# Head products copied raw and split inside the first FFN; W1 and W2 loaded where their low halves lie

## The chip, the cores and the metric

One core of a Trainium2 chip runs one program. The metric is the device time of one execution in microseconds (us), the median of several runs. The engines are named as in the profile: PE (TensorE), DVE (VectorE), ACT (ScalarE), POOL (GpSimd) and SP (SyncE, which here only issues transfers).

## The reference, cut to what matters

4096 rows of 128 numbers pass an FFN with top-1 routing over 8 experts, an attention with 8 heads over 512 keys, and the same FFN again:

```python
x = x + 0.5 * ffn(layernorm(x), gate_w, gate_b, expert_bias, w1, b1, w2, b2)
x = x + attn(layernorm(x), context, Wq, Wk, Wv, Wout, bout)
x = x + 0.5 * ffn(layernorm(x), ...)
# ffn: e = argmax(x @ gate_w.T + gate_b + expert_bias)
#      relu(x @ w1[e] + b1[e]) @ w2[e] + b2[e]           (128 -> 512 -> 128)
# attn, per head: q = x @ Wq, k = context @ Wk, v = context @ Wv,
#      softmax(sharpened q @ k.T / sqrt(128)) @ v, then @ Wout + bout
```

## The kernel before

**Two halves of every factor.** All products that matter are made in three matmuls of a faster format: each factor is split in a high half (a copy, by ACT, into that format) and a low half (factor minus high half, by DVE or POOL), and `three` adds high x high, high x low and low x high. So W1 (8 experts of 128x512), W2 (the same size, its halves interleaved in `w2_hi_lo`) and two products per head are split once. Per head, PE first transposes Wq, Wk and Wv (`head_transposes`), multiplies the weights (`head_weights`) and then with the context: M of head h (`head_products`, 128x512, in one bank of PSUM) stands for the head's keys seen through Wq, VW (128x512, in another bank) for its values seen through Wout. The attention takes only M and VW.

**Stages.** (1) Up to about 36 us: x is loaded, its row statistics and gate logits are made, rows are ranked by expert and a table says which row lies in which of the 39 slots (128 rows of one expert each). (2) PE makes M and VW of heads 0 to 5 between its routing matmuls; ACT copies the high halves out of the banks, DVE subtracts. (3) The first FFN, a pipeline of 39 slots: in its step m, PE transposes the hidden rows of slot m-3 (L1448), multiplies those of slot m-4 with W2 (L1460, L1463), transposes slot m (L1470) and multiplies slot m-1 with W1 (`three`); ACT copies (L711, L718, L723) and normalises slot m+1 (L701); DVE adds b1 (L1140) and b2 (L1143), adds the result up (L1149) and makes low halves (L1157, L1162). POOL gathers the rows of slot j+7 (L514, an indirect transfer) and then adds the second part of slot j's result (L523), in iteration j. SP stores each finished slot, one after the other, and loads groups of rows back. Heads 6 and 7 are made in steps 0 and 1. (4) The attention, 256 units in 8 groups. (5) The second FFN.

**What sets the order.** Every engine runs one list in the order of the program text, and semaphores tie the lists. Before the change:

- M and VW of a head stay in their banks until DVE has made both low halves from them; PE's next head of the same bank waits for that (`wait_bank`). The first two heads are copied a second time (`keep`) into the later half of b1's place, so that load of b1 waits too.
- Wq, Wk, Wv and Wout lie in the place of experts 4 to 7 of `w2_hi_lo`. W1 and W2 share the buffer `w_raw`: W2 of an expert is loaded once W1's low half is made (`load_w2`), the first four of those by POOL (L534), the other four by DVE (L1037).
- PE's step 1 waits for all low halves of W1, for those of heads 0 to 5, and for `packed_ready`, the end of a small table on DVE (`packed_rows`, L968 to L975). Its step 4 waits for all low halves of W2 (L1042), which DVE makes in steps 1 to 3, behind ACT's high halves (L647).
- DVE's step 2 waits for b1 and for b2, halved by L1174 in step 1.

The list of DVE between the routing and the FFN, in the kernel's words:

```python
head(LOW_ORDER[0])
rows_of_slots()
experts_of_tiles()
for h in LOW_ORDER[1:5]:
    head(h)
for e in range(POOL_LOWS, E):
    w1_low(e)
head(LOW_ORDER[5])
packed_rows()
```

## Time and profile before

| | before |
|---|---|
| runs | 761.33, 761.49, 762.7 us; median 761.49 |
| profiled execution | 759.55 us, span 757.8 us, so 1.75 us lie outside the span |
| granted TensorE clock, mean | 0.983 |
| busy share of the span | PE 94%, DVE 80%, ACT 65%, POOL 46% |
| matmul instructions | 4374 |
| DVE instructions | 1663 |

Start times are microseconds from the span's start. A duration in a timeline row is that of one instruction, or from the first to the end of the last where the row says xN; neighbours on DVE and ACT overlap a little, so that what an instruction costs in a queue is the distance to the next start. "idle before" names what ended the idle time. PEclk is the share of full clock that was granted to PE. In the kernel an instruction is named by its tile: `w_lo` is the low half of W1, `w_hi_lo` that of W2, `bank` any bank of PSUM, `xn_then_xnT_or_oT` in L1174 the place of b2.

### The profile page before, as it was taken

To read this page: it belongs to the slowest core of one execution; us is meant where nothing else is said; L and a number is where in the kernel's file an instruction comes from. 1 tells how busy PE (TensorE), PEld (TensorE's weight loads), DVE (VectorE), ACT (ScalarE), POOL (GpSimd) and SP (SyncE) were. 2 spreads that over 40 slices of the span, in tenths; PEclk is the share of its full clock that TensorE was granted. 3 is DMA by queue.
4 is the path that set the end of the run, shared out by engine and by line. 5 is a ranking of instruction groups with operands and counts; after the bars stand their busy time and mean duration, and the time that the engine had idled before them with its cause. 6 is when DMAs were issued, how large, how long until landed. Compare 5 with 4: busy or idle time off the path is not lost.

```text
span 757.8 us, 15224 instructions
## 1 busy us (share of the span) xinstructions
PE 716.0 (94%) x4374; PEld 600.7 (79%) x4374; DVE 608.8 (80%) x1663; ACT 492.8 (65%) x1199; POOL 351.2 (46%) x482
## 2 busy tenths in 40 slices
PE   9967999899999999999999999999999999789993
PEld 7756899778888878878878888887887887669992
DVE  7998888887777878788788787787878877588883
ACT  3755666577677667667767767766766665446661
POOL 4072666244334345346345445534534533266663
PEclk9989999999999999999999999999999999899997
DMA  9770333210000000000000000000000011222210
GB/s 254 270 199 20 84 81 84 58 43 2 1 1 1 1 5 11 1 2 14 1 1 11 5 2 8 8 0 4 12 2 1 15 43 53 102 76 65 58 49 9
DMA packets 31792, 31.49 MB, mean 42 GB/s; under 512 B 5049, under 2 KB 26183, under 8 KB 31200
## 3 DMA queue, kind: packets, MB, share of 16 engines
q1 hardware_dynamic: 27360, 23.91, 10.6%
q0 software_dynamic: 3520, 6.40, 3.3%
q8 instruction: 38, 0.62, 0.4%
q14 instruction: 42, 0.34, 0.2%
q10 hardware_dynamic: 832, 0.21, 0.1%
HBM read 20.96 MB, written 10.47 MB: 41 GB/s over the span
## 4 chain that ended last, share of the span: by engine, by line
PE 58%; DVE 26%; issue 8%; DMA 3%; POOL 2%; DVEq 2%; ACT 1%; POOLq 0%; SPq 0%; ACTq 0%
PE bank L1409 14%; PE bank L1411 14%; PE bank L1410 14%; PE bank L1619 13%; DVE hT_lo L1157 5%; DVE neg_max L1297 3%; DVE slot_rows L1143 2%; DVE probsT_lo L1303 2%; DVE slot_rows L1149 2%; DVE slot_xT_lo L1162 2%; DMA b<-in_L_ffn_b 1%; DMA rows<-in_L_attn_x 1%; POOL rows L553 1%; DVE h L1140 1%; PE bank L1660 1%
## 5 line engine op out<-in xcount | busy, mean ns | idle before, releaser
L569 POOL TENSOR_SCALAR probs<-probs,row_inv 128x512 f32<-128x512 f32 x256 | 178.4, 697 | 274.6 <-DVE row_inv L1308 273.3
L760 ACT ACTIVATE probs<-bank,neg_max 128x512 f32<-128x512 f32 x256 | 176.3, 689 | 143.6 <-DVE neg_max L1297 142.5
L1297 DVE TENSOR_REDUCE neg_max<-bank 128x1 f32<-128x512 f32 x256 | 176.5, 690 | 85.7 <-PE bank L1411 83.2
L1303 DVE TENSOR_TENSOR probsT_lo<-bank,probsT_hi 128x512 fp32r<-128x512 f32 x256 | 174.4, 681 | 2.2 <-ACT probsT_hi L769 2.0
L1619 PEld LDWEIGHTS bank<-ident,probs 128*128 128x128 f32 x1024 | 127.2, 140 | 37.1 <-POOL probs L569 1.0
L1619 PE MATMUL bank<-ident,probs 128*128 128x128 f32 x1024 | 153.4, 272 | 0.5 <-DVE probsT_lo L1303 0.3
L769 ACT ACTIVATE probsT_hi<-bank 128x512 fp32r<-128x512 f32 x256 | 151.1, 590 | 2.1 <-PE bank L1619 2.1
L1409 PE MATMUL bank<-m_hi,xT_hi 128*128 128x512 f32 x256 | 122.3, 478 | 1.4 <-ACT probs L760 1.4
L1409 PE MATMUL bank<-probsT_hi,vw_hi 128*128 128x512 f32 x256 | 101.7, 397 | 4.0 <-DVE probsT_lo L1303 4.0
L1410 PE MATMUL bank<-probsT_lo,vw_hi 128*128 128x512 f32 x256 | 101.5, 396 | 0.0
L1411 PE MATMUL bank<-probsT_hi,vw_lo 128*128 128x512 f32 x256 | 101.5, 396 | 0.0
L1410 PE MATMUL bank<-m_lo,xT_hi 128*128 128x512 f32 x256 | 100.8, 394 | 0.0
L1411 PE MATMUL bank<-m_hi,xT_lo 128*128 128x512 f32 x256 | 100.6, 393 | 0.0
L1460 PE MATMUL bank<-w_hi_lo,hT_hi 128*128 x312 | 82.7, 342 | 6.8 <-DVE hT_lo L1157 5.1
L1140 DVE TENSOR_TENSOR h<-bank,b 128x512 f32<-128x512 f32 x78 | 53.9, 691 | 19.8 <-PE bank L1411 14.1
L1463 PE MATMUL bank<-w_hi_lo,hT_lo 128*128 x312 | 69.3, 222 | 0.0
L1460 PEld LDWEIGHTS bank<-w_hi_lo,hT_hi 128*128 128x128 f32 x312 | 58.7, 188 | 10.3 <-issue 10.2
L718 ACT ACTIVATE hT_hi<-bank 128x512 fp32r<-128x512 f32 x78 | 46.7, 599 | 29.9 <-PE bank L1448 29.1
L1409 PEld LDWEIGHTS bank<-probsT_hi,vw_hi 128*128 128x128 f32 x256 | 48.0, 188 | 18.7 <-DVE probsT_lo L1303 7.7
L1463 PEld LDWEIGHTS bank<-w_hi_lo,hT_lo 128*128 128x128 f32 x312 | 59.6, 191 | 0.0
L1411 PEld LDWEIGHTS bank<-m_hi,xT_lo 128*128 128x128 f32 x256 | 48.1, 188 | 11.2
L514 POOL DMA_INDIRECT slot_rows<-x_stats,row_of_slot x39 | 40.8, 1046 | 34.6 <-issue 34.6
(222 smaller groups left out, 1241.7 us busy)
## 6 DMA issues: line engine op xcount, KB each, us to landing
w_raw<-in_L_ffn_w SPq DMA_DIRECT2D x16, 256.0 KB, 6.7
b<-in_L_ffn_b SPq DMA_DIRECT2D x4, 1024.0 KB, 6.2
x_packed<-slot_rows SPq DMA_DIRECT2D x39, 65.5 KB
slot_rows<-slots SPq DMA_DIRECT2D x39, 65.5 KB, 1.8
x_stats<-rows SPq DMA_DIRECT2D x4, 524.0 KB, 10.4
rows<-x_packed SPq DMA_DIRECT2D x8, 262.0 KB, 3.5
rows<-in_L_attn_x SPq DMA_DIRECT2D x4, 512.0 KB, 8.1
slot_rows<-x_stats,row_of_slot POOLq DMA_INDIRECT x39
```

The source lines that it names most:

```text
L569: pool.tensor_scalar(PR[:, u % 4, :], PR[:, u % 4, :], RI[:, u % 4:u % 4 + 1], 1.0, ALU.mult, ALU.mult).then_inc(normed, 1)
L760: act.activation(PR[:, n % 4, :], BK[n % 2][:, :], ACT.Exp, bias=NM[:, n % 4:n % 4 + 1], accum_out=SU[:, n % 4:n % 4 + 1]).then_inc(probs, 1)
L769: act.activation(PTH[:, (u // G) % 2, :, (u % G) * P:(u % G + 1) * P], BK[2 + u % 2][:, :].rearrange("p (c q) -> p c q", c=KC), ACT.Copy)\
L1140: v.tensor_tensor(HB[:, j % 3, :].unsqueeze(1), BK[2 + j % 2][:, :].unsqueeze(1), B1[:, ds(e, 1), :], ALU.add).then_inc(s_hb, 1)
L1297: v.tensor_reduce(NM[:, n % 4:n % 4 + 1], BK[n % 2][:, :], AX.X, ALU.max, negate=True)\
L1303: v.tensor_tensor(PTL[at], BK[2 + u % 2][:, :].rearrange("p (c q) -> p c q", c=KC), PTH[at].bitcast(fp32), ALU.subtract).then_inc(pT_lo, 1)
L1409: pe.matmul(out_, wh, mh, start=start, stop=False)
L1410: pe.matmul(out_, wh, ml, start=False, stop=False)
L1411: return pe.matmul(out_, wl, mh, start=False, stop=stop)
L1460: pe.matmul(BK[6 + j % 2][:, 0:2 * D].rearrange("p (a s d) -> p a s d", a=1, s=2), HTH[:, j % 2, c * P:(c + 1) * P], W2HL[:, ds(e, 1), c, ...
L1463: last = pe.matmul(BK[6 + j % 2][:, 0:D].unsqueeze(1), HTL[:, j % 2, c * P:(c + 1) * P], W2HL[:, ds(e, 1), c, 0, :], start=False, stop=(c ...
L1619: last = pe.transpose(BK[2 + u % 2][:, c * P:(c + 1) * P], PR[:, u % 4, c * P:(c + 1) * P], IDN[:, :])
```

## The change

The raw products of a head are copied by ACT from the banks into `m_raw` and `vw_raw`, which lie at the addresses of `m_lo` and `vw_lo`; the banks come free with these copies. The halves are made later, from SBUF: from step 7 of the first FFN on, every second step, ACT makes one high half (`head_high`: M of head 0 in step 7, VW of head 0 in step 9, M of head 1 in step 11), DVE the low half of M a step later (`m_low`, steps 8, 12 to 36), POOL that of VW (`vw_low`, after the add of slots 5, 9 to 33). The second copy and its place are gone. The attention's first unit waits for all of them.

W1 is loaded into the place of its low halves and W2 into that of its own, interleaved; the low half is then written over the raw one. So W2 and both halves of b1 are loaded behind the row statistics with no wait, `w_raw` is gone, and the attention's weights take its room. DVE makes all eight low halves of W1, halves b2 and makes two of W2 before the FFN; ACT makes four high halves of W2 before it. The small table is cut in two: its first two instructions (`empty_slots`) stay ahead of W1's low halves, the last four come in DVE's step 3. PE's step 1 waits for the copies of heads 0 to 5, for those two instructions and for W1's low halves; its step 4 for W2's.

```diff
+        with ExitStack() as products_at:
+            MRAW = sb("m_raw", [P, H, KEYS], fp32, products_at)
+            VWRAW = sb("vw_raw", [P, H, KC * D], fp32, products_at)
         ML = sb("m_lo", [P, H, KEYS], f32r)
-        VWH = sb("vw_hi", [P, H, KC, D], f32r)
         VWL = sb("vw_lo", [P, H, KC, D], f32r)
...
-            WRAW = sb("w_raw", [P, E, F], fp32, prep)
+            HEADS = sb("wq_wk_wv_wout", [P, 4, H * D], fp32, prep)
...
-        KEPT = [[B1_PLACE[:, E // 2 + 2 * h + k, :] for k in range(2)] for h in range(2)]
+        W1RAW = W1L[:, :, :].bitcast(fp32)
+        W2RAW = W2HL[:, :, :, 1, :].bitcast(fp32)
...
-        LOW_ORDER = [2, 0, 1, 3, 4, 5, 6, 7]
-        POOL_LOWS = 4
...
+        SPLIT_STEP = 7
+
+        def split_at(m, lag):
+            k, odd = divmod(m - lag - SPLIT_STEP, 2)
+            return [divmod(k, 2)] if not odd and 0 <= k < 2 * H else []
+
+        def wait_bank(eng, bank, h, which):
 
             before = [k for k in range(h) if bank[k] == bank[h]]
-            if before and before[-1] < len(KEPT):
+            if before:
                 eng.wait_ge(head_kept, 2 * before[-1] + which)
-            elif before:
-                eng.wait_ge(low, lows_until(before[-1]))
...
             for c in range(NCH):
                 store_stats(c)
+            for e in range(E):
+                load_w2(e)
             load_b1(0)
+            load_b1(1)
             sp.wait_ge(place_ps, NCH)
             load_b2(0)
-            sp.wait_ge(m_lo, max(lows_until(h) for h in range(len(KEPT))))
-            sp.wait_ge(vw_lo, max(lows_until(h) for h in range(len(KEPT))))
-            load_b1(1)
-            for e in range(E):
-                load_w2(e)
...
+            def vw_low(h):
+                pool.wait_ge(head_hi, 2 * h + 2)
                 apart(pool, pool_passed)
+                pool.tensor_tensor(VWL[:, h, :, :].rearrange("p c d -> p (c d)"), VWRAW[:, h, :],
+                                   VWH[:, h, :, :].rearrange("p c d -> p (c d)").bitcast(fp32), ALU.subtract)\
+                    .then_inc(vw_lo, 1)
 
             LEAD = 7
             for j in range(LEAD):
                 gather(j)
-                if j == 1:
-                    for e in range(POOL_LOWS):
-                        w1_low(e)
             for j in range(SLOTS):
                 gather(j + LEAD)
                 add_low(0, j)
+                for h, part in split_at(j + 5, 1):
+                    if part == 1:
+                        vw_low(h)
...
+            def keep(h, part):
+                act.wait_ge((m_ps, vw_ps)[part], h + 1)
+                act.activation((MRAW, VWRAW)[part][:, h, :], BK[(M_BANK, VW_BANK)[part][h]][:, :], ACT.Copy)\
+                    .then_inc(head_kept, 1)
+
+            def head_high(h, part):
+                act.wait_ge(head_kept, 2 * h + part + 1)
+                if part == 0:
+                    act.activation(MH[:, h, :], MRAW[:, h, :], ACT.Copy).then_inc(head_hi, 1)
+                else:
+                    act.activation(VWH[:, h, :, :].rearrange("p c d -> p (c d)"), VWRAW[:, h, :], ACT.Copy)\
+                        .then_inc(head_hi, 1)
...
             def w2_high(e):
-                act.wait_ge(w_in[e], 32)
+                act.wait_ge(w2_in, 16 * E)
...
             def head(h):
-                products(h)
+                keep(h, 0)
+                keep(h, 1)
                 if h + 1 < H:
                     ww_evac(h + 1)
-                if h < len(KEPT):
-                    keep(h)
                 if h + 2 < H:
                     wT_evac(h + 2)
...
+            for e in range(4):
+                w2_high(e)
...
-                    if r == 0 and 0 < m < 4:
-                        if m == 2:
-                            act.wait_ge(wT_ps, H)
-                            act.wait_ge(ww_ps, H)
-                        if m == 1:
-                            w2_high(0)
-                            w2_high(1)
-                        w2_high(2 * m)
-                        w2_high(2 * m + 1)
                     if r == 0 and m < 2:
                         head(BEFORE_FFN + m)
+                        w2_high(4 + 2 * m)
+                        w2_high(5 + 2 * m)
+                    if r == 0:
+                        for h, part in split_at(m, 0):
+                            head_high(h, part)
...
-            head(LOW_ORDER[0])
             rows_of_slots()
             experts_of_tiles()
-            for h in LOW_ORDER[1:5]:
-                head(h)
-            for e in range(POOL_LOWS, E):
+            empty_slots()
+            for e in range(E):
                 w1_low(e)
-            head(LOW_ORDER[5])
-            packed_rows()
+            half_b2(0)
+            w2_low(0)
+            w2_low(1)
...
-                    if r == 0 and m < 2:
-                        head(LOW_ORDER[BEFORE_FFN + m])
...
+                    if r == 0 and m < 3:
+                        for e in range(2 + 2 * m, 4 + 2 * m):
+                            w2_low(e)
+                    if r == 0 and m == 3:
+                        packed_rows()
+                    if r == 0:
+                        for h, part in split_at(m, 1):
+                            if part == 0:
+                                m_low(h)
...
                     if r == 0 and m == 1:
-                        pe.wait_ge(vw_lo, lows_until(BEFORE_FFN - 1))
-                        pe.wait_ge(packed_ready, 1)
-                        pe.wait_ge(w1_lo_first, POOL_LOWS)
-                        pe.wait_ge(w1_lo, E - POOL_LOWS)
-                    if r == 0 and m == 2:
-                        pe.wait_ge(m_lo, lows_until(BEFORE_FFN - 1))
+                        pe.wait_ge(head_kept, 2 * BEFORE_FFN)
+                        pe.wait_ge(table_step[0], EMPTY_LINKS)
+                        pe.wait_ge(w1_lo, E)
...
+                    if u == 0:
+                        pe.wait_ge(m_lo, H)
+                        pe.wait_ge(vw_lo, H)
```

DVE, from the experts of the slots (`expert_of_tile`) to the first instruction of FFN step 0 (`slot_xT_lo`), before:

```order
L923 TENSOR_SCALAR expert_of_tile<-tile_f 128x39
L1050 TENSOR_TENSOR m_lo<-b_place,m_hi 128x512
L1053 TENSOR_TENSOR vw_lo<-b_place,vw_hi 128x512
...
L1037 TENSOR_TENSOR w_lo<-w_raw,w_hi 128x512 x4
L1050 TENSOR_TENSOR m_lo<-bank,m_hi 128x512
L1053 TENSOR_TENSOR vw_lo<-bank,vw_hi 128x512
L968 TENSOR_SCALAR counts<-counts 128x8
L969 TENSOR_TENSOR counts<-counts,bank 128x8
L970 TENSOR_TENSOR sel<-sel,counts 128x312
L972 TENSOR_REDUCE tile_f<-sel 128x39
L973 SCALAR_TENSOR_TENSOR tile_f<-tile_index,tile_f 128x39
L975 TENSOR_SCALAR packed_row_of_tile<-tile_f 128x39
L1162 TENSOR_TENSOR slot_xT_lo<-bank,slot_xT_hi 128x128
```

and now:

```order
L917 TENSOR_SCALAR expert_of_tile<-tile_f 128x39
L962 TENSOR_SCALAR counts<-counts 128x8
L963 TENSOR_TENSOR counts<-counts,bank 128x8
L1035 TENSOR_TENSOR w_lo<-w_lo,w_hi 128x512 x8
L1050 TENSOR_SCALAR xn_then_xnT_or_oT<-xn_then_xnT_or_oT 128x1024
L1040 TENSOR_TENSOR w_hi_lo<-w_hi_lo 128x4x128 x2
L1156 TENSOR_TENSOR slot_xT_lo<-bank,slot_xT_hi 128x128
```

All head halves have left this stretch (two more stood ahead of the first row shown), four halves of W1 and two of W2 and the halving of b2 have come, and four instructions of the table have left.

ACT, from the last work on a head before the FFN to the first rows of step 0, before:

```order
L620 ACTIVATE wqT_wkT_wvT<-bank 128x320
L701 ACTIVATE slot_xn<-slot_rows 128x128
L723 ACTIVATE slot_xT_hi<-bank 128x128
L701 ACTIVATE slot_xn<-slot_rows 128x128
L632 ACTIVATE m_hi<-bank 128x512
```

and now:

```order
L616 ACTIVATE wqT_wkT_wvT<-bank 128x320
L645 ACTIVATE w_hi_lo<-w_hi_lo 128x4x128 x4
L699 ACTIVATE slot_xn<-slot_rows 128x128
L721 ACTIVATE slot_xT_hi<-bank 128x128
L699 ACTIVATE slot_xn<-slot_rows 128x128
L628 ACTIVATE m_raw<-bank 128x512
```

Four high halves of W2 now stand ahead of the first slot's normalising.

POOL, around the add of slot 5 (`y_lo_half` is the part added), now:

```order
L518 TENSOR_TENSOR slot_rows<-slot_rows,y_lo_half 128x128
L529 TENSOR_TENSOR vw_lo<-vw_raw,vw_hi 128x512
L509 DMA slot_rows<-x_stats,row_of_slot 128x131
L518 TENSOR_TENSOR slot_rows<-slot_rows,y_lo_half 128x128
L509 DMA slot_rows<-x_stats,row_of_slot 128x131
L518 TENSOR_TENSOR slot_rows<-slot_rows,y_lo_half 128x128
```

Before, adds and gathers alternated here with nothing between; the low half of VW now stands ahead of the gather of slot 13, and so again every fourth iteration.

## Rows read from the trace of the kernel before

**Rows 1.** table of stretches: us, busy us of each engine (instructions), PEclk, DMA share, GB/s

```profile
41.00:46.00 5.00, 4.88 (x23) 4.06 (x23) 5.00 (x4) 2.39 (x5) 4.84 (x5) 0.66 0.92 285
52.00:57.00 5.00, 4.94 (x17) 3.26 (x16) 3.87 (x8) 4.08 (x10) 1.80 (x2) 0.66 0.40 97
66.00:85.00 19.00, 19.00 (x144) 17.37 (x143) 16.70 (x45) 12.70 (x36) 11.56 (x16) 1.00 0.21 48
```

**Rows 2.** timeline, DVE: start us, us, line, operation, out<-in, count [idle before]

```profile
36.06 0.19 DVE L958 TENSOR_SCALAR row_of_slot_f<-bank 128x39 f32<-128x39 f32 x1
...
42.09 0.67 DVE L1053 TENSOR_TENSOR vw_lo<-bank,vw_hi 128x512 fp32r<-128x512 f32 x1
...
42.69 5.33 DVE L1037 TENSOR_TENSOR w_lo<-w_raw,w_hi 128x512 fp32r<-128x512 f32 x4
...
49.53 0.48 DVE L970 TENSOR_TENSOR sel<-sel,counts 128x312 f32<-128x312 f32 x1
...
50.79 0.18 DVE L975 TENSOR_SCALAR packed_row_of_tile<-tile_f 128x39 int32<-128x39 f32 x1
...
57.40 0.68 DVE L1174 TENSOR_SCALAR xn_then_xnT_or_oT<-xn_then_xnT_or_oT 128x1024 f32<-128x1024 f32 x1
```

**Rows 3.** timeline, POOL, before the FFN, and line L1037 by itself

```profile
37.84 1.26 POOL L514 DMA_INDIRECT slot_rows<-x_stats,row_of_slot  x1 [19.78 <-issue]
...
40.66 5.00 POOL L534 TENSOR_TENSOR w_lo<-w_raw,w_hi 128x512 fp32r<-128x512 f32 x4
...
L1037 DVE TENSOR_TENSOR w_lo<-w_raw,w_hi x4: 678/679/3527, 42.7 to 47.3; 128x512 fp32r<-128x512 f32 x4
```

**Rows 4.** timeline, PE: two idle stretches, and the FFN from step 4

```profile
41.12 1.10 PE L1553 MATMUL bank<-ctxT_sharp,wk_wqT_and_wv_wout 96*128 96x512 f32 x2 [2.73 <-DVE m_lo L1050]
...
51.63 0.30 PE L1470 MATMUL bank<-ident,slot_xn 128*128 128x128 f32 x1 [3.05 <-issue]
...
64.44 0.38 PE L1460 MATMUL bank<-w_hi_lo,hT_hi 128*128 x1 [1.48 <-DVE w_hi_lo L1042]
...
66.25 0.60 PE L1448 MATMUL bank<-ident,h 128*128 128x128 f32 x4
```

**Rows 5.** timeline, ACT: slot 0 normalised, then the first four high halves of W2

```profile
45.51 0.48 ACT L701 ACTIVATE slot_xn<-slot_rows 128x128 f32<-128x128 f32 x1
...
52.59 2.17 ACT L647 ACTIVATE w_hi_lo<-w_raw 128x512 fp32r<-128x512 f32 x4
```

**Rows 6.** timeline, one settled FFN step: DVE, PE, ACT and POOL

```profile
70.88 0.69 DVE L1140 TENSOR_TENSOR h<-bank,b 128x512 f32<-128x512 f32 x1 [0.25 <-PE bank L1411]
...
71.49 0.28 DVE L1143 TENSOR_TENSOR slot_rows<-slot_rows,xn_then_xnT_or_oT 128x128 f32<-128x128 f32 x1
...
71.89 0.68 DVE L1157 SCALAR_TENSOR_TENSOR hT_lo<-bank,hT_hi 128x512 fp32r<-128x512 f32 x1
...
73.04 0.36 PE L1460 MATMUL bank<-w_hi_lo,hT_hi 128*128 x1
...
72.35 0.49 ACT L701 ACTIVATE slot_xn<-slot_rows 128x128 f32<-128x128 f32 x1
...
73.32 0.60 ACT L718 ACTIVATE hT_hi<-bank 128x512 fp32r<-128x512 f32 x1 [0.32 <-PE bank L1448]
...
70.83 1.02 POOL L514 DMA_INDIRECT slot_rows<-x_stats,row_of_slot  x1 [0.38 <-issue]
...
72.19 0.41 POOL L523 TENSOR_TENSOR slot_rows<-slot_rows,y_lo_half 128x128 f32<-128x128 f32 x1 [0.35 <-DVE slot_rows L1149]
```

**Rows 7.** DMA view of 0 to 130 us: GB/s in 40 slices of 3.25 us

```profile
GB/s 55 224 292 299 297 381 297 378 418 273 5 161 50 355 306 278 150 0 3 0 0 41 66 50 51 74 65 166 70 63 134 62 61 142 46 76 124 68 71 120
```

**Rows 8.** timeline, POOL, late in the FFN, and line L1143 by itself

```profile
121.15 1.02 POOL L514 DMA_INDIRECT slot_rows<-x_stats,row_of_slot  x1 [0.66 <-issue]
...
L1143 DVE TENSOR_TENSOR slot_rows<-slot_rows,b x39: 281/283/508, 651.5 to 741.7; 128x128 f32<-128x128 f32 x39
```

**Rows 9.** timeline, DVE, round 7 of the attention

```profile
161.32 0.30 DVE L1090 BATCH_NORM_STATS2 bn<-rows 128x6 f32<-128x128 f32 x1 [0.59 <-DMA rows<-x_packed]
```

92 lines of the change are left out of this document (29 added, 63 removed).

## The prediction

> **What bounds the kernel now.** I read the table of stretches first, since the change touches only the start of the program. In the settled FFN (66 to 85 us) PE is busy in all 19.00 of 19 us at full clock [rows 1]: a step there takes PE's 2.14 us, and nothing that comes earlier at a step's start makes it shorter. Before that, PE runs at 0.66 of full clock in two stretches that follow idle ones [rows 1], and the timelines say why it is idle. It waits 2.73 us for a low half of M before head 5, and 3.05 us before slot 1 [rows 4]: "issue" stands there, but this is step 1, whose last wait is for the small table, and DVE ends that at 50.79 + 0.18 = 50.97 [rows 2]. The first product with W2 (step 4) comes at 64.44 behind a low half of W2, and step 5, the first of regular shape, at 66.25 [rows 4]. So the head of the program is bound by DVE's list, and the change rewrites that list. It cannot gain after 66.25; there it can only add.
>
> **DVE ahead of the FFN.** Low halves follow each other every 42.69 - 42.09 = 0.60 us [rows 2]. From the slot table at 36.06 to 50.97 DVE takes 14.9 us. Removed: five heads' low halves, 10 x 0.60 = 6.0; the last four instructions of the small table, 1.44 from 49.53 to 50.97; and a blocked instruction. That is L1037: four of them take 5.33 us, one alone 3527 ns against 678 [rows 3], so 2.85 us are lost while POOL makes its four low halves of W1 (40.66 to 45.66, rows 3). The Trainium skill ("SBUF — State Buffer", Who interferes with whom) says that a DVE instruction with two SBUF inputs and a GpSimd instruction that reads SBUF exclude each other for a whole instruction; by that rule, the trace agrees. POOL's four are gone, so the block is too. Added: four low halves of W1 and two of W2, 6 x 0.60 = 3.6, and L1174, about 0.6 [rows 2]. The two low halves ahead of 36.06 go as well, but there DVE then waits for PE's placing matmuls; of the 1.2 us (the bounds are 0 and 1.2) I take 0.5. So W1's low halves are done at 35.56 + 1.8 (slot and expert table) + 0.4 + 8 x 0.60 = 42.6, and DVE reaches step 0 at 44.4, not 50.97.
>
> **PE and ACT take the lead.** With the banks freed by ACT's copies, head 5 starts 2.73 us earlier, and 0.24 us more from head 4's wait (an estimate). If PE is not slow there, it is also about 1.2 us shorter. ACT then stands ahead of slot 0 at 45.51 - 2.97 - 1.2 = 41.3 [rows 5], makes four high halves of W2, 2.17 us [rows 5], and normalises slot 0 at 43.5. PE transposes it at 44.2, does head 6 (about 2.3 us at full clock) and starts step 1 at 46.5: DVE's 42.6 no longer holds it. That is 5.1 us earlier than 51.63. ACT copies head 6 until 46.8, makes two more halves of W2 until 48.2; DVE follows with its low halves and adds b1 for slot 0 at 50.1; with two low halves in step 2 and the rest of the table in step 3 I come to 53.7 for PE's step 4 and 57.1 for step 5, against 66.25: 9.1 us earlier. DVE is then some 0.5 us behind for the next step, so **8.6 us** come out of the head.
>
> **What takes some of it back.**
> - *Clock.* The walk above has PE at full clock, but PE still idles some 2 us before slot 0, and idle stretches are followed by slow ones now: 5 us at 0.66 are about 3.4 us at half clock, 1.7 us of work lost [rows 1]. One such stretch would fall on heads 6 and 7, on the path; the others are partly hidden behind DVE. Between 0 and 3.4 us I take **1.3**.
> - *Loads.* Transfers end in the tenth slice, at 32.5 us, after 378 and 418 GB/s [rows 7]. W2 and the second half of b1, 3.15 MB, now come behind them: at about 380 GB/s 8.3 us, until 40.8, and b2, issued at 35.5, after that, at about 42.5, when DVE wants it. The gather of slot 0 starts by 37.3 and shares the engines with them; ACT wants it at 43.5. Between 0 and 2 us I take **0.3**.
> - *POOL in the FFN.* This is the new cost, paid eight times. A low half takes POOL 5.00 / 4 = 1.25 us [rows 3]. Its settled step is 1.02 us of gather, 0.4 of add and two gaps, 0.38 and 0.35 [rows 6]; the second is a wait for DVE, so it can catch up about 0.33 us a step, 1.3 in four, just what one low half takes. The gather behind it starts about 1.3 us late. The gather of slot 9 starts at 70.83, and ACT uses it one step behind the row at 72.35, at 74.49: 3.66 us. Late in the FFN gathers start 0.33 us later (the gap of 0.66 at 121.15, rows 8) and hold nobody up, so they land within 3.33. Late by 1.3, one holds ACT for 1.0; ACT's own idle of 0.32 before L718 [rows 6] and the time between the end of DVE's hT_lo, 71.89 + 0.68 = 72.57, and PE's use of it at 73.04 [rows 6], about 0.4 without the signal, take 0.7 to 0.8 of this. PE is left with a stall of 0.2 to 0.3 for each of the seven that stand ahead of a gather: with bounds of 0 and 10.9 (rival 4) I take **2.0**.
> - *DVE and ACT in the FFN cost nothing.* A low half of M, 0.60, every fourth step meets 0.25 us of DVE's idle time a step [rows 6] and the 0.4 above; a high half on ACT, about 0.5 every second step, meets idle gaps of 0.32 and about 0.4. If that cover were gone, DVE would lose 8 x 0.35 = 2.8 us.
> - *SP.* Stores queue one behind the other, and the last group of rows comes just late for the attention: DVE waits 0.59 us for it in round 7 [rows 9]. SP starts as much earlier as the FFN does, but a late add delays a store: **0.2**.
>
> **The sum.** 8.6 - 1.3 - 0.3 - 2.0 - 0.2 = 4.8 us. The profiled execution took 759.55 us (span 757.8 and 1.75 outside), the median of the runs is 761.49, 1.94 more; from 759.55 I get 754.75, and on the scale of the median **756.7 us**.
>
> **The rivals.**
> 1. *Nothing is given back.* Gathers land early enough and PE keeps its clock: 8.6 less 0.6 for loads and SP, 753.5. For it: gathers within 3.33 us. Against: PE still idles before slot 0.
> 2. *The loads take the place of the wait.* If W2, b1 or b2 come 4 us later than I have it (b2 is 0.5 MB in a queue of 3.15), DVE stands in front of them with everything behind it: 756.7 + 3 = about 759.5. For it: the margin at b2 is none. Against: W2 is wanted only at 41.3.
> 3. *The block moves into the FFN.* POOL's low half reads SBUF for 1.25 us, and L1143 of DVE has two SBUF inputs in every step. That they do exclude each other shows in the second FFN: 508 ns at most against 283 [rows 8]. In my timing POOL's half lies from 2.1 us of a step to 1.2 of the next, and L1143 at 0.95 loses 0.3, within the slack. If the phase is worse, DVE stands for the full 1.25, less 0.4 of slack, eight times: 6.8 us in place of 2.0, and the result is 761.5, no change. The rule of the Trainium skill named above asks for no more than that: whichever instruction starts first holds the other for its length.
> 4. *Slower: POOL becomes the bound.* One mechanism: the gather behind each low half. Four steps of POOL are 4 x (1.02 + 0.4 + 0.38) + 1.25 = 8.5 us against PE's 8.56. If signals make a gap of 0.3 around each low half (gaps without work are 0.38 now), it is 8.8, the lateness is never caught up, and if gathers land only just in time, each of the seven costs its full 1.25 + 0.3 = 1.55: 10.9 in place of 2.0, that is 765.6 us. It decides against the change once a low half costs more than (4.8 + 2.0) / 7 = 0.97 us. Against it: the 0.33 us of rows 8 that held nobody up.
> 5. *The change doesn't do what it says*: PE's step 1 stays gated by another wait. The list shows only copies, two table instructions and W1's halves there, all done by 42.6; that would leave about 761.5.
>
> **The chances.** My forecast (a gain of 3 to 8 us) 0.58, rival 1 0.15, rival 2 0.10, rival 3 0.07, rival 4 0.08, rival 5 0.02. A difference of 0.2%, 1.5 us, is about what a measurement of this kernel tells from none. The first three are faster, 0.83; rivals 3 and 5 make 0.09 for the same, rival 4 0.08 for slower. The range goes from rival 1 with a microsecond of luck at the placing matmuls, 752.5, to the far end of rival 2 and the better half of rival 3, 760.9; outside lie rival 4 and the rest of rival 3, under 0.2.
>
> **What would show it.** In the changed profile: PE's first product with W2 near 55 us and not 64.44; no instruction of L1035 (low half of W1) above 0.7 us; L529 (`vw_lo` on POOL) eight times in the FFN, of 1.25 us each; DVE's L1137 (b2's add) at most some 0.3 us above 0.28; ACT's slot_xn waiting for the gather once every four steps, by about 1 us, and PE losing 0.2 to 0.3 us behind it; the attention's first matmul 5 us earlier and everything after it unchanged in length. I am wrong if PE's step 5 comes after 60 us (then loads or ACT bound the head), or if the FFN from there on takes over 5 us longer than now (then POOL bounds the FFN).

## The result, and the profile after

The changed kernel takes **754.64 us** (median of 4 runs, 754.38 to 755.23) against 761.41 for the kernel before beside it (4 runs, 759.75 to 762.7): a ratio of 0.9909, with a 95% interval of 0.9888 to 0.993. The forecast was 756.7 us, 752.5 to 760.9. Run again beside the last three experiments, the ratio was 0.9935 (0.9909 to 0.996). So it is faster, by 0.4% to 1.1%.

The profiled execution took 754.72 us, 4.83 less than the profiled one of before; the forecast on that scale was 4.8 less. Between the medians it is 6.8 us, and 6.4 the second time.

| | before | after |
|---|---|---|
| median of the runs, us | 761.41 | 754.64 |
| profiled execution, us | 759.55 | 754.72 |
| its span, us | 757.8 | 752.9 |
| first product with W2 (step 4), us | 64.44 [rows 4] | 55.95 |
| transposes of h in step 6, us | 68.39 | 61.44 |
| the same in step 41 (the last tile), us | 144.46 | 139.89 |

The last two rows are the measure for everything below. PE's four transposes of h stand once in every step, so their start dates a step. How much earlier they start than in the profile of before is called the **lead**: after the change it is 6.95 us in step 6 and 4.57 in step 41. The head of the program gives about 7, and the FFN gives 2.38 of it back. Two limits of this measure: each lead comes from one execution, and steps 17 to 19 of the profile of before hold a stall of their own. There the transposes stand 2.65 and 2.36 us apart instead of 2.14, 0.73 too much in all, while ACT waits 1.43 us for a gather beside the 458 KB transfer `fill`. A kernel that stalls there as long keeps its lead, and one that doesn't stall gains 0.73.

The transposes of h in steps 6 and 41, PE's timeline of the kernel before (start us, us, line, operation):

```profile
68.39 0.60 PE L1448 MATMUL bank<-ident,h 128*128 128x128 f32 x4
...
144.46 0.62 PE L1448 MATMUL bank<-ident,h 128*128 128x128 f32 x4
```

The same view of the changed kernel, with slot 0, step 1, the first W2 product and step 5 (L1450 was L1460, L1438 was L1448):

```profile
44.35 0.33 PE L1460 MATMUL bank<-ident,slot_xn 128*128 128x128 f32 x1 [2.36 <-ACT slot_xn L699]
...
47.66 0.42 PE L1460 MATMUL bank<-ident,slot_xn 128*128 128x128 f32 x1
...
55.95 0.58 PE L1450 MATMUL bank<-w_hi_lo,hT_hi 128*128 x1 [0.22 <-DVE hT_lo L1151]
...
59.23 0.66 PE L1438 MATMUL bank<-ident,h 128*128 128x128 f32 x4
61.44 0.60 PE L1438 MATMUL bank<-ident,h 128*128 128x128 f32 x4
...
139.89 0.62 PE L1438 MATMUL bank<-ident,h 128*128 128x128 f32 x4
```

These answer to rows 4: the wait of 2.73 us for a low half of M and the one of 3.05 ahead of step 1 are gone. What stands in their place is a wait of 2.36 us for ACT's first slot.

DVE's timeline of the changed kernel, from the slot table on:

```profile
38.07 4.91 DVE L1035 TENSOR_TENSOR w_lo<-w_lo,w_hi 128x512 fp32r<-128x512 f32 x8
43.89 0.69 DVE L1050 TENSOR_SCALAR xn_then_xnT_or_oT<-xn_then_xnT_or_oT 128x1024 f32<-128x1024 f32 x1 [0.92 <-DMA xn_then_xnT_or_oT<-in_L_ffn_b]
...
49.51 0.29 DVE L1156 TENSOR_TENSOR slot_xT_lo<-bank,slot_xT_hi 128x128 fp32r<-128x128 f32 x1 [2.33 <-ACT slot_xT_hi L721]
```

Eight low halves of W1 take 4.91 us where four of them took 5.33 [rows 2]: nobody shuts DVE out. They end at 42.98, and from then on DVE waits for others.

ACT's timeline of the changed kernel, ahead of slot 0 and at its longest wait for a gather (tile 16):

```profile
41.73 2.19 ACT L645 ACTIVATE w_hi_lo<-w_hi_lo 128x512 fp32r<-128x512 f32 x4
43.81 0.49 ACT L699 ACTIVATE slot_xn<-slot_rows 128x128 f32<-128x128 f32 x1
...
83.84 0.49 ACT L699 ACTIVATE slot_xn<-slot_rows 128x128 f32<-128x128 f32 x1 [1.22 <-DMA slot_rows<-x_stats,row_of_slot]
```

The table of stretches of the changed kernel (us, PE busy, PEclk, DMA share, GB/s), which answers to rows 1:

```profile
41.00:44.00 3.00, 0.99 (x10) 1.00 0.70 256
44.00:50.00 6.00, 5.65 (x21) 0.72 0.21 47
50.00:56.00 6.00, 4.08 (x26) 0.99 0.05 11
56.00:62.00 6.00, 6.00 (x34) 0.72 0.01 1
66.00:85.00 19.00, 18.94 (x142) 1.00 0.35 81
```

PE is granted less than full clock twice: from 44 to 50 us (head 6 and the start of head 7), and from 56 to 62 us (steps 4 and 5).

In the FFN, two of GpSimd's low halves and the gathers behind the first (POOL's timeline of the changed kernel):

```profile
72.03 1.28 POOL L529 TENSOR_TENSOR vw_lo<-vw_raw,vw_hi 128x512 fp32r<-128x512 f32 x1
73.46 1.02 POOL L509 DMA_INDIRECT slot_rows<-x_stats,row_of_slot  x1 [0.15 <-issue]
...
75.09 1.02 POOL L509 DMA_INDIRECT slot_rows<-x_stats,row_of_slot  x1 [0.16 <-issue]
...
76.77 1.29 POOL L509 DMA_INDIRECT slot_rows<-x_stats,row_of_slot  x1 [0.16 <-issue]
...
79.18 1.02 POOL L509 DMA_INDIRECT slot_rows<-x_stats,row_of_slot  x1 [0.34 <-issue]
80.23 0.42 POOL L518 TENSOR_TENSOR slot_rows<-slot_rows,y_lo_half 128x128 f32<-128x128 f32 x1
80.60 1.28 POOL L529 TENSOR_TENSOR vw_lo<-vw_raw,vw_hi 128x512 fp32r<-128x512 f32 x1
```

Behind a low half gathers start 1.63 and 1.68 us apart, not 2.14: POOL works off about 0.5 us of its delay in a step, and the third gather (76.77) is nearly on time. In steps 6 to 16 the lead stays between 6.95 and 6.97 although two low halves ran there (the two shown). It then falls in a few places: 6.67 in step 17, 6.35 in step 19, 5.95 and 5.65 in steps 30 and 31, 5.29 in step 35, 4.99 in step 39, 4.57 in step 41.

### The profile page after: what moved, and what is told of

It reads as the page before. It is cut to its first block, busy times and chain, and to the rows that moved or that the text cites. A ratio compares the mean times of both kernels' runs of the same rounds, so it can differ in the third digit from the quotient of the medians.

```text
span 752.9 us, 15236 instructions
## 1 busy us (share of the span) xinstructions
PE 716.0 (95%) x4374; PEld 600.2 (80%) x4374; DVE 604.1 (80%) x1659; ACT 496.9 (66%) x1211; POOL 357.5 (47%) x486
## 4 chain that ended last, share of the span: by engine, by line
PE 71%; DVE 13%; DMA 5%; issue 4%; POOL 2%; ACT 1%; DVEq 1%; SPq 0%; POOLq 0%; ACTq 0%
PE bank L1403 15%; PE bank L1405 15%; PE bank L1404 15%; PE bank L1612 13%; DMA x_packed<-slot_rows 4%; PE bank L1450 3%; DVE neg_max L1291 3%; DVE probsT_lo L1297 2%; PE bank L1438 2%; DVE hT_lo L1151 2%; PE bank L1453 1%; DMA b<-in_L_ffn_b 1%; POOL rows L549 1%; PE bank L1352 1%; PE bank L1653 1%
## 5 line engine op out<-in xcount | busy, mean ns | idle before, releaser
L1450 PE MATMUL bank<-w_hi_lo,hT_hi 128*128 x312 | 83.5, 345 | 6.3 <-DVE hT_lo L1151 6.1
L1450 PEld LDWEIGHTS bank<-w_hi_lo,hT_hi 128*128 128x128 f32 x312 | 59.1, 190 | 11.1 <-issue 10.7
L1134 DVE TENSOR_TENSOR h<-bank,b 128x512 f32<-128x512 f32 x78 | 53.7, 688 | 14.2 <-PE bank L1405 9.3
L716 ACT ACTIVATE hT_hi<-bank 128x512 fp32r<-128x512 f32 x78 | 46.5, 596 | 23.5 <-PE bank L1438 23.4
L1405 PEld LDWEIGHTS bank<-probsT_hi,vw_lo 128*128 128x128 f32 x256 | 48.1, 188 | 10.9
## 6 DMA issues: line engine op xcount, KB each, us to landing
x_stats<-rows SPq DMA_DIRECT2D x4, 524.0 KB, 10.2
```

The lines of the kernel that those rows point to most:

```text
L1134: v.tensor_tensor(HB[:, j % 3, :].unsqueeze(1), BK[2 + j % 2][:, :].unsqueeze(1), B1[:, ds(e, 1), :], ALU.add).then_inc(s_hb, 1)
L1405: return pe.matmul(out_, wl, mh, start=False, stop=stop)
L1450: pe.matmul(BK[6 + j % 2][:, 0:2 * D].rearrange("p (a s d) -> p a s d", a=1, s=2), HTH[:, j % 2, c * P:(c + 1) * P], W2HL[:, ds(e, 1), c, ...
```

## The experiments

My first theory had two parts. The head gains from both halves of the change, DVE's freed list (for step 1) and the early W2 (for step 4). The FFN gives back what GpSimd's low halves make the gathers late. Rivals: one half of the change is the whole gain; ACT's and DVE's splits or SBUF's ports are what costs in the FFN.

Runs e5 to e8 were made on a chip on which the kernel before took some 8 us more (769.88), so they are compared by ratio and by lead. "Outside 17 to 19" is what is given back without the steps at `fill` (the lead in step 16 less that in step 19 is left out).

| run | median, us | ratio to before, 95% | lead, step 6 | lead, step 41 | given back | outside 17 to 19 | ACT's waits for gathers, 60 to 140 us |
|---|---|---|---|---|---|---|---|
| after | 754.64 | 0.9909 (0.9888 to 0.993) | 6.95 | 4.57 | 2.38 | 1.76 | 2.5 |
| e9, the same again | 754.70 | 0.9935 (0.9909 to 0.996) | 7.91 | 6.74 | 1.17 | 1.16 | 3.4 |
| e1 deferral alone | 754.71 | 0.9905 (0.9888 to 0.9921) | 5.64 | 4.54 | 1.10 | 1.55 | 4.0 |
| e2 loads alone | 761.66 | 0.9992 (0.9979 to 1.0005) | -1.54 | -1.36 | -0.18 | -0.01 | 1.5 |
| e3 without VW's low halves | 753.89 | 0.9901 (0.988 to 0.9923) | 8.72 | 8.38 | 0.34 | 0.34 | 2.0 |
| e4 these on DVE | 753.04 | 0.9886 (0.9866 to 0.9907) | 7.22 | 5.66 | 1.56 | 0.97 | 2.3 |
| e5 no split in the FFN | 760.95 | 0.9883 (0.9851 to 0.9916) | 8.52 | 8.89 | -0.37 | 0.26 | 1.2 |
| e6 eight tiles ahead | 762.34 | 0.9903 (0.9876 to 0.993) | 7.43 | 5.55 | 1.88 | 2.38 | 0.0 |
| e7 low half twice | 767.55 | 0.9979 (0.9956 to 1.0003) | 5.76 | -1.29 | 7.05 | 6.41 | 10.2 |
| e8 before, eight ahead | 767.92 | 0.9974 (0.9965 to 0.9984) | -0.32 | 0.13 | -0.45 | -0.01 | 0.0 |
| e10 DVE, eight ahead, earlier | 752.83 | 0.9895 (0.9879 to 0.9912) | 7.51 | 7.37 | 0.14 | 0.24 | 0.0 |
| e11 and W2 behind the slots | 756.42 | 0.995 (0.9932 to 0.9968) | 5.46 | 4.94 | 0.52 | 1.19 | 0.0 |
| e12 idle time filled | 755.94 | 0.9943 (0.9923 to 0.9963) | 8.48 | 6.80 | 1.68 | 1.95 | 3.1 |

In the profile of before ACT's waits for gathers are 1.4 us. These waits don't tell what is given back: the changed kernel has 2.5 us of them and gives back 2.38, its second profile (e9) 3.4 and 1.17. The column outside steps 17 to 19 orders the kernels better. With GpSimd's low halves once per head it holds 1.2 to 2.4 us; in e3 and e5, which have none, and in e10 0.2 to 0.3. But e4 and e11, with these halves on DVE, have 1.0 and 1.2.

**e1, the deferral alone.** From the changed kernel; W1 and W2 come through their own buffer as before, and W2's halves are made in steps 1 to 3 as before (cut to what matters):

```diff
-W1RAW = W1L[:, :, :].bitcast(fp32)
-W2RAW = W2HL[:, :, :, 1, :].bitcast(fp32)
+W1RAW = WRAW
 def load_w2(e):
+    sp.wait_ge(w1_lo, e + 1)
```

> The changed kernel with the loads put back: the heads' products are still copied raw and split inside the FFN, but W1 goes through its own buffer again, each W2 load waits for a W1 low half, and W2's high and low halves stand in steps 1 to 3 as before the change. Theory (both parts are needed, the freed list of DVE for step 1 and the early W2 for step 4): DVE reaches W1's low halves at 38 us, so step 1 stays near 47 to 48, but the eight W2 loads leave only from 39 to 43 us and the first W2 product comes near 59 to 61 us (after the change 55.95, before 64.44); the time lies 1 to 3 us below the kernel before. Rival A (the deferral is the whole gain): first W2 product within 0.5 us of 55.95, time 6 to 7 us below before. Rival B (the early loads are the whole gain): step 5 at 66 us as before, and the time 2 us above before, since the splits in the FFN still cost.

**e2, the loads alone.** From the kernel before (cut to what matters):

```diff
+W1RAW = W1L[:, :, :].bitcast(fp32)
+W2RAW = W2HL[:, :, :, 1, :].bitcast(fp32)
 def load_w2(e):
-    if e < POOL_LOWS:
-        sp.wait_ge(w1_lo_first, e + 1)
-    else:
-        sp.wait_ge(w1_lo, e - POOL_LOWS + 1)
```

> The kernel before with the loads alone changed: W1 and W2 are loaded straight into the places of their low halves, W2 right behind the statistics' stores; the heads' products are split ahead of the FFN as before, GpSimd makes four of W1's low halves. Theory (both parts are needed): step 1 stays at 51 to 52 us, since DVE's list is untouched; W2 is there, so steps 2 to 4 lose their waits for it and step 5 starts 2 to 4 us earlier than 66.25; nothing is given back in the FFN, so the time lies 2 to 4 us below before. Rival A (the deferral is the whole gain): within 0.5 us of before. Rival B (the early loads are the whole gain): 6 to 9 us below before.

Both came out for rival A, and the first part of my theory fell. The deferral alone gives the changed kernel's time (7.4 us below before); the loads alone give a ratio whose interval includes 1. The rows say why. PE's timeline of e1:

```profile
55.88 0.58 PE L1460 MATMUL bank<-w_hi_lo,hT_hi 128*128 x1 [1.54 <-DVE w_hi_lo L1049]
...
59.15 1.05 PE L1448 MATMUL bank<-ident,h 128*128 128x128 f32 x4
```

The first W2 product stands at 55.88, not at 59 to 61 as I expected, and within 0.07 us of the changed kernel's. That it is so close is in part chance. In e1 this product waits for DVE's low halves of W2; in the changed kernel it comes behind a stretch at 0.72 of full clock, and where that program kept full clock it stands at 54.54 (e3) and 55.34 (e9). So the early loads, with the halves of W2 that they let stand ahead of the FFN, may be worth 0.5 to 1.3 us at this point; the times don't show it. Once DVE makes W1's low halves from 38 us on, the W2 loads that wait for them still land before ACT wants them. DVE's timeline of e2:

```profile
42.74 5.28 DVE L1029 TENSOR_TENSOR w_lo<-w_lo,w_hi 128x512 fp32r<-128x512 f32 x4
...
53.18 2.50 DVE L1034 TENSOR_TENSOR w_hi_lo<-w_hi_lo 128x512 fp32r<-128x512 f32 x4 [0.61 <-ACT w_hi_lo L642]
```

With W2 long in place, its first low halves start at 53.18; in the kernel before:

```profile
53.24 1.29 DVE L1042 TENSOR_TENSOR w_hi_lo<-w_raw,w_hi_lo 128x512 fp32r<-128x512 f32 x2 [0.67 <-ACT w_hi_lo L647]
```

Nearly the same moment, and the same wait. They wait for ACT's high halves, and those for the order of the list. And DVE is shut out of SBUF here as before (5.28 us for four). So in the kernel before the wait for W2 in rows 4 is not a wait for its load. e1's lead in step 6 is 1.3 us smaller than the changed kernel's, with the first W2 product at the same place: from 56 to 62 us its PE was granted 0.50, the changed kernel's 0.72.

**e3, without GpSimd's low halves of VW** (attention reads the high half instead):

```diff
-for h, part in split_at(j + 5, 1):
-    if part == 1: vw_low(h)
```

> The changed kernel without GpSimd's eight low halves of VW; attention takes VW's high half in their place, so its TensorE work is the same. Theory (GpSimd's 1.28 us low halves put the gathers behind them late, and that is what the FFN gives back): the FFN's steps keep their lead of 6.95 us over the kernel before through to step 41, less 0.3 at most, and the time lies 1.8 to 2.5 us below the changed kernel. Rival (the splits on ACT and DVE, m's low half beside a gather, or the DMA queues are what costs): within 0.5 us of the changed kernel, with the stalls at steps 17 to 19, 30, 31, 33, 35 and 39 to 41 still there.

The lead falls by 0.34 us only, and in step 39 for most of it; the expectation for the steps holds nearly to the letter. Of the time I expected 1.8 to 2.5 us less: the profiled span is 2.8 less (750.1 against 752.9), but 1.8 of that is clock ahead of the edit, and the medians are 0.75 apart with overlapping intervals. So what speaks is the lead of one execution: 0.34 given back, where four profiles with the low halves (after, e9, e1, e12) have 1.1 to 2.4.

**e4, VW's low halves on DVE:** `(m_low, vw_low)[part](h)` in DVE's step, nothing on GpSimd.

> The changed kernel with VW's low halves made by DVE (two steps behind their high halves, as m's are) and none by GpSimd; the output is the reference's. Theory (GpSimd's queue is the cost and DVE has the room): 8 x 0.65 us go into DVE's slack, the gathers stand on time, and the time lies 1.2 to 2.3 us below the changed kernel. Rival (DVE has no room in a step of 2.14 us): 8 x 0.35 us are added and the give-back of 2.3 goes, so the time is 0 to 0.8 us above the changed kernel; steps 9, 13, 17 and so on then take 2.5 us.

Given back 1.56 us, less than the 2.38 of the changed kernel but more than e9's 1.17. So the low halves on GpSimd are not the whole cost. Neither account is right in its detail: steps 9 and 13 do not grow as the rival has it; instead 0.6 went at the 458 KB transfer of `fill` (slot_xn of tile 17 waits 1.97 us, step 18 takes 3.19 us), and 0.6 in step 41, behind the last low half.

**e5, no split in the FFN at all:** ACT copies straight into `m_hi` and `vw_hi`, and the 16 high and 16 low halves are gone (attention reads high halves for the low ones).

> The changed kernel with no split of the heads at all inside the FFN: ACT's copies out of PSUM go straight into the high halves, neither ACT's 16 high copies nor DVE's eight low halves of M nor GpSimd's eight of VW are there, and attention takes the high half in place of the low one, so its TensorE work is the same. Theory (GpSimd's low halves are nearly the whole give-back): within 0.4 us of the kernel without VW's low halves, 1.8 to 2.7 us below the changed kernel. Rival (the other two thirds of the splits cost too): 0.5 us or more below the kernel without VW's low halves.

Nothing is given back, 0.37 is even gained, 0.7 us more than in e3, which looks like the rival's. But 0.63 of it arises in steps 17 to 19. At `fill` ACT waits 0.82 us for a gather in e5 and 1.42 in e3 (84.43), for a gather that was issued on time, at 81.40, with no split beside it. Outside these steps the two differ by 0.08. The times cannot tell them apart (the intervals of the ratios overlap). What does differ can be seen at other gathers. The gather of tile 11 in e3, POOL's timeline, and DVE's low half of M beside it:

```profile
66.12 0.68 DVE L1042 TENSOR_TENSOR m_lo<-m_raw,m_hi 128x512 fp32r<-128x512 f32 x1
...
66.39 1.30 POOL L509 DMA_INDIRECT slot_rows<-x_stats,row_of_slot  x1 [0.33 <-issue]
```

In e5 the same gather takes 1.02 us, as all 31 of the FFN do; in e3 seven of them take 1.27 to 1.39.

**e6, the gathers eight tiles ahead:** `LEAD = 8`.

> The changed kernel with the gathers issued eight tiles ahead instead of seven; everything else as it is. Theory (a gather behind a low half lands too late for ACT's slot_xn): one more step of 2.14 us ahead covers 1.28 us, ACT's waits for the gathers go, and the time lies 1.5 to 2.3 us below the changed kernel. Rival (the stalls come from SBUF port contention or from a slower DMA in that stretch, not from the gathers' lateness): within 0.4 us of the changed kernel.

As the theory says, ACT's waits for gathers go (0.0 us), and the lead, 7.43 in step 6, gains what before loses at `fill` and is still 7.84 in step 31. By step 34 it is 7.43 again, and 0.96 us go in one blow from step 36 to 37. At the end 1.88 are given back all the same, and the ratio is the changed kernel's. DVE's, POOL's and PE's timelines of e6:

```profile
125.03 1.54 DVE L1137 TENSOR_TENSOR slot_rows<-slot_rows,xn_then_xnT_or_oT 128x128 f32<-128x128 f32 x1
...
125.12 1.29 POOL L529 TENSOR_TENSOR vw_lo<-vw_raw,vw_hi 128x512 fp32r<-128x512 f32 x1
...
127.51 0.38 PE L1450 MATMUL bank<-w_hi_lo,hT_hi 128*128 x1 [0.69 <-DVE hT_lo L1151]
```

DVE's addition of b2, two SBUF inputs, 0.28 us of work, lasts until POOL's low half is over. This is rival 3 of the prediction. It is there in the changed kernel too, milder, and it costs. In step 40 (POOL, DVE and PE of the changed kernel):

```profile
136.22 1.28 POOL L529 TENSOR_TENSOR vw_lo<-vw_raw,vw_hi 128x512 fp32r<-128x512 f32 x1
...
136.95 0.70 DVE L1137 TENSOR_TENSOR slot_rows<-slot_rows,xn_then_xnT_or_oT 128x128 f32<-128x128 f32 x1
...
138.92 0.38 PE L1450 MATMUL bank<-w_hi_lo,hT_hi 128*128 x1 [0.22 <-DVE hT_lo L1151]
```

The addition is 0.42 us too long, and the lead falls by 0.42 in the next step. It does so in e9 too (0.42, behind an addition of 0.69); in e3, e5 and e10 the lead stands still there. (Line L1137 by itself: count, then ns least/median/most.)

```profile
L1137 DVE TENSOR_TENSOR slot_rows<-slot_rows,xn_then_xnT_or_oT x39: 273/282/697, 51.5 to 139.3; 128x128 f32<-128x128 f32 x39
```

**e7, each low half twice** (into a buffer nobody reads):

```diff
+                apart(pool, pool_passed)
+                pool.tensor_tensor(AGAIN[:, :], VWH[:, h, :, :].rearrange("p c d -> p (c d)").bitcast(fp32),
+                                   VWH[:, h, :, :].rearrange("p c d -> p (c d)").bitcast(fp32), ALU.subtract)
```

> The changed kernel with each of GpSimd's low halves of VW followed by a second subtraction of the same size into a spare buffer (its result is used nowhere). Theory (what counts is how late the next gathers are): the next gather is 2.6 us late instead of 1.3, each of the seven that a gather follows costs 1 to 1.5 us, and the time is 5 to 10 us above the changed kernel. Rival (the give-back has another cause than GpSimd's queue): 1 us or less above it.

7.05 us are given back, 4.7 more than in the changed kernel, and ACT's waits for gathers, 2.5 us in the changed kernel, are 10.2 (lines by ACT between 60 and 140 us: busy us, mean ns, then idle us ahead and its releasers). First the changed kernel, then e7:

```profile
L699 ACT ACTIVATE slot_xn<-slot_rows 128x128 f32<-128x128 f32 x33 | 16.1, 489 | 2.5 <-DMA slot_rows<-x_stats,row_of_slot 2.5
```

```profile
L703 ACT ACTIVATE slot_xn<-slot_rows 128x128 f32<-128x128 f32 x33 | 16.2, 491 | 13.3 <-DMA slot_rows<-x_stats,row_of_slot 10.2 <-issue 2.8
```

The cost grows much faster than the dose: 1.28 us in every fourth step nearly fits, another 1.09 does not. Over before no gain is left that the interval shows (0.9979, up to 1.0003). This run shows that lateness of the gathers can cost; how much of the changed kernel's 2.38 it is, it does not show.

**e8, the kernel before with eight tiles ahead.**

> The kernel before with the gathers issued eight tiles ahead instead of seven. Theory (the gathers are late only behind GpSimd's low halves, which this kernel has not): within 0.4 us of the kernel before, or up to 0.8 us below it if the slow steps 18 and 19 (2.65 and 2.36 us, at the time of the 458 KB fill) were gathers too. Rival (a gather issued earlier is worth something in any case): 1.5 us or more below.

In the lead 0.45 us, all at the `fill` transfer, as the theory has it. But the ratio is 0.9974 (0.9965 to 0.9984), 2.0 us, which meets the rival's number. There is no profile of before on that chip to compare with, so where the rest comes from is open. What eight tiles ahead gain here, with no low half on GpSimd, may be in e10's time too.

**e9 to e12**, run beside each other. e9 is the changed kernel. e10 takes VW's low halves to DVE, `LEAD = 8`, `SPLIT_STEP = 5`. e11 is e10 with W2's high halves in steps 0 to 2 (`(range(0, 2), range(2, 5), range(5, 8))[m]`), the low ones behind them, and b2's halving in step 1. e12 is the changed kernel with 22 instead of 6 idle products at slot 0.

> The changed kernel once more, beside the three below on the same chip: the measure for them. Theory (the TensorE clock of the first FFN steps is granted by chance from run to run, as the profiles of the kernels without VW's low halves and of this one differ ahead of any edit): its time stands 0.990 to 0.992 of the kernel before, and its profile may show step 6 anywhere from 59.7 us (clock 1.00 throughout) to 62.7 us (clock 0.50 from 53 to 62 us).

> The changed kernel with the three edits that the runs so far speak for: VW's low halves on DVE instead of GpSimd, gathers eight tiles ahead instead of seven, the splits begun at step 5 instead of 7 (so that the last stands clear of the FFN's last steps). Theory (what the FFN gives back is gathers late behind GpSimd's low halves, and DVE's bias addition shut out of SBUF by them, 1.54 us instead of 0.28 in the run with eight ahead): no DVE bias addition above 0.35 us in the FFN, no wait of ACT for a gather above 0.2 us after step 10, the lead over before at step 41 at least as large as at step 6, and the time 2 to 3 us below the changed kernel. Rival (DVE has no room for the eight more): within 0.7 us of the changed kernel.

> The kernel with VW's low halves on DVE and eight tiles ahead, and besides W2's high halves on ACT moved behind the first slots' normalisations (two in step 0, three in step 1, three in step 2, none ahead of the FFN), W2's low halves one step each behind them, b2's halving in step 1. Theory (the changed kernel's first slot waits for four high halves of W2 that are needed only in step 4, and the early W2 loads bought nothing so): slot_xn 0 at 41.5 us instead of 43.8, first W2 product at 52 to 54 us instead of 55.95 at full clock, and the time 1 to 2.5 us below the run beside it without this edit. Rival (what sets the first W2 product is the sum of ACT's and DVE's work on the halves, wherever it stands): within 0.5 us of that run.

> The changed kernel with 22 instead of 6 idle products of ones on TensorE while it waits for the first slot (2.36 us of idle there after the change). Theory (the half clock that TensorE was granted from 44 to 50 us follows on that idle stretch): clock 1.00 from 44 to 50 us, step 3 at 50.0 to 50.6 us instead of 51.7, the lead at step 6 up to 1.7 us larger, and the median 0.5 to 1.7 us below the changed kernel. Rival (the clock is granted without regard to this stretch, since one run kept it at 1.00 through the same idle time): the clock still falls in the profile or the median is within 0.4 us of the changed kernel.

*e9, the clock and b2.* The same program, other profile: PE keeps full clock all through the head, step 6 comes at 60.48, and the lead is 7.91. The table of stretches of e9:

```profile
44.00:50.00 6.00, 4.91 (x27) 1.00 0.26 65
50.00:56.00 6.00, 4.07 (x25) 1.00 0.01 1
56.00:62.00 6.00, 5.29 (x39) 1.00 0.04 14
```

and of e7, which runs the same instructions up to step 6:

```profile
44.00:50.00 6.00, 5.98 (x19) 0.50 0.22 47
50.00:56.00 6.00, 4.53 (x23) 0.95 0.04 11
56.00:62.00 6.00, 5.54 (x30) 0.72 0.01 1
```

Seven profiles have the changed kernel's instructions up to step 6 (after, e3, e4, e5, e6, e7, e9; in e5 ACT's copies go to another place, and e6 has one more gather). PE waits 2.36 us for slot 0 in all of them, and is then at full clock in three (e3, e5, e9) and not in four. Step 6 starts between 59.67 (e3) and 62.63 us (e7): 2.96 us of spread with nothing changed ahead of it. The Trainium skill ("TensorE: Matmul & The Clock Gate", Part 1) says that how many matmuls run slow differs from run to run of one kernel; these runs agree.

Not all of the spread is the clock. e3 and e9 both have full clock throughout, and step 6 is 0.81 us later in e9. There b2 came late. DVE's and PE's timelines of e9:

```profile
45.49 0.69 DVE L1050 TENSOR_SCALAR xn_then_xnT_or_oT<-xn_then_xnT_or_oT 128x1024 f32<-128x1024 f32 x1 [2.71 <-DMA xn_then_xnT_or_oT<-in_L_ffn_b]
...
47.73 0.50 PE L1403 MATMUL bank<-w_hi,slot_xT_hi 128*128 x1 [0.96 <-DVE slot_xT_lo L1156]
```

DVE stands 2.71 us for b2, with the first slot's low half behind it, and PE waits 0.96 us for that half. In e3 DVE stands 1.85 us and PE 0.20. b2 lands 3.5 us after its issue in the kernel before and in e1, where W2 comes behind it, and 8.0 to 9.8 in the changed kernel, e3 and e9, where W2 is ahead of it. So the early loads do cost something: 0.8 us in e9, nothing in the first profile, where ACT was later still.

*e12* does show 1.00 in these three stretches and a lead of 8.48, as the theory wants, but its median is 755.94 against 754.70. One profile at full clock proves nothing where three of seven had it anyway, and the times show no gain. So whether an idle stretch ahead decides the clock is not settled here; filling it is worth nothing that these times show. Its profile is also one in which the rest of the program takes 1.9 us more than that of before: the lead in step 41 is 6.80, the profiled time only 4.93 less.

*e10* does what the second part of the theory says. The lead goes from 7.51 to 7.37, and the 0.26 us lost in step 39 are there in every kernel with the deferral (0.23 to 0.44), in e5 with 0.23. ACT waits for no gather, and no addition of b2 is shut out any more (views as above):

```profile
L696 ACT ACTIVATE slot_xn<-slot_rows 128x128 f32<-128x128 f32 x33 | 16.0, 485 | 0.0
```

```profile
L1140 DVE TENSOR_TENSOR slot_rows<-slot_rows,xn_then_xnT_or_oT x39: 280/282/299, 51.6 to 136.6; 128x128 f32<-128x128 f32 x39
```

Its median is 752.83 (752.31 to 752.99, 4 runs), 1.9 us below the changed kernel beside it, with a ratio of 0.9895 (0.9879 to 0.9912) against 0.9935 (0.9909 to 0.996); the intervals overlap a little. The three edits were made together; each one's share is not measured, and no gain over e4 shows, whose ratio is 0.9886. Nor is it shown that VW's halves are free on DVE: eight tiles ahead alone gained e8 2.0 us, and e11, with the same three edits, gives back 1.19 us outside steps 17 to 19.

*e11* was meant to take away the wait of 2.36 us for slot 0 and is 3.6 us slower than e10. DVE's timeline of e11:

```profile
50.10 1.90 DVE L1036 TENSOR_TENSOR w_hi_lo<-w_hi_lo 128x512 fp32r<-128x512 f32 x3 [1.23 <-ACT w_hi_lo L642]
51.92 0.69 DVE L1052 TENSOR_SCALAR xn_then_xnT_or_oT<-xn_then_xnT_or_oT 128x1024 f32<-128x1024 f32 x1
53.36 0.69 DVE L1133 TENSOR_TENSOR h<-bank,b 128x512 f32<-128x512 f32 x1 [0.76 <-DVE xn_then_xnT_or_oT L1052]
```

and PE behind it:

```profile
54.11 0.69 PE L1436 MATMUL bank<-ident,h 128*128 128x128 f32 x2 [4.14 <-DVE h L1133]
```

Slot 0 came at 43.29 and not at 41.5, since ACT then waited 1.69 us for its gather. And I had put three low halves of W2 and b2's halving ahead of DVE's first addition of b1: all wait in one queue for ACT's third to fifth high half, and PE for all of them. Neither account had this.

## Why the prediction was right, and where not

In the order of its steps, with the head at full clock from e3 and the rest from the first profile of the changed kernel: head 8.7 (forecast 8.6), clock -1.8 (-1.3), FFN -2.4 (-2.0), loads 0 (-0.3), the rest +0.3 (-0.2), in all 4.8 to 4.9 (4.8). The second profile (e9) has the same head, no clock loss, loads -0.8, FFN -1.2, the rest +0.5, in all 7.2. So the gain came where it was forecast, and the size of each term behind the head is that of one execution; that they add up to 4.8 in the first is luck. Several steps were off.

- **The head: right.** The walk was made at full clock, and e3 shows it at full clock: step 1 at 46.45 (forecast 46.5), step 4 at 53.66 (53.7), the first W2 product at 54.54 ("near 55"), step 5 at 56.98 (57.1), the lead in step 6 8.72. DVE's eight low halves end at 42.98 (42.6), slot 0 is normalised at 43.81 (43.5). e1 and e2 show that the deferral makes nearly all of it; the prediction had given the early loads no gain of their own, and the times of e1 and e2 show none.
- **The clock: the sum right, its nature wrong.** 1.3 was taken for one stretch behind an idle one. The first profile has two, for 61.44 - 59.67 = 1.77 us, but it differs from run to run: nothing in e3, e5 and e9, 2.96 us in e7. It belongs in the range as a spread, not in the sum as a term. What grants the full clock after the same wait in one run and not in another is open.
- **POOL in the FFN: the amount right, the way half right.** e3 and e7 show that GpSimd's low halves cost, but not that they are all of it (e4). I had "a stall of 0.2 to 0.3 for each of the seven", and a POOL that works off 0.33 us in a step; it works off 0.5. The second low half cost nothing and the lead fell in few places: at `fill` (1.22 us of waiting for tile 16, whose gather started at 79.18, only some 0.3 late, beside the 458 KB issued at 79.82; before waits there too), behind blocked additions of b2, and elsewhere. The second profile of the same kernel gives back 1.17, half of the first. So 2.0 lies between the 1.2 and 2.4 of the two profiles, and is no price per gather.
- **The block in the FFN: named, priced at zero, wrong.** "L1137 at most some 0.3 us above 0.28" was passed twice in the changed kernel (0.69 and 0.70), and in e6 it was 1.26 above. It cost 0.42 us in step 41 of the changed kernel and 0.96 in step 37 of e6. Rival 3 is real, and rests on where POOL's low half falls in DVE's step: with one tile more ahead the longest addition went from 0.4 above to 1.26. The Trainium skill ("SBUF — State Buffer", Who interferes with whom) says that whichever instruction is issued first holds the other for its whole length. e6 agrees that DVE was held to the end, its instruction ended 0.16 us behind POOL's; but DVE's row starts 0.09 us ahead of POOL's, so the start times don't tell who holds whom.
- **DVE and ACT in the FFN at nothing: borne out.** e5 against e3 puts it at 0.08 us outside steps 17 to 19; the other 0.6 comes with ACT's wait for one gather at `fill`, which differs between kernels without any split there too (1.43 us in before, 0.82 in e5).
- **The loads: named, and right in size for two runs.** DVE waited 0.92 us for b2 (43.89) in the first profile, but ACT's slot 0 was later anyway; in e9 it waited 2.71, and PE lost 0.8. This is rival 2 in small: "the margin at b2 is none" was right.
- **From the profile to the median.** "On the scale of the median" I added 1.94 us, the distance of before. The profile of before was one of its faster executions, that of after was not (754.72 against a median of 754.64). So 4.83 for a forecast of 4.8 compares two single executions, and is luck in part; the gain between medians, 6.8 and then 6.4 us, is 1.6 to 2.0 more than forecast. (Rival 1's "0.6 for loads and SP" is 0.5 by the terms named, 0.3 and 0.2.)

What the second run of the same kernel (ratio 0.9935 after 0.9909) leaves open is how much of the 6.8 us is the change and how much luck: the lead at the end of the FFN says 4.6 to 6.7, against one profile of before.
